# Attention stage: four PSUM banks for the scores and three in the ring of units, in place of three and four

## What is computed

```python
qkv = einsum('bnc,dc->bnd', xn, qkv_w) + qkv_b       # q, k, v: 16 heads of 32
attn = softmax(einsum('bhqd,bhkd->bhqk', q, k) * 32**-0.5)
out = einsum('bhqk,bhkd->bhqd', attn, v)             # then the output projection
return x + attention(xn) + experts(xn)
```

## Time and profile before

| | us |
|---|---|
| median of three runs | 4841.46 |
| the profiled execution, its own time | 4836.55 |
| span of its trace | 4834.7 |
| TensorE matmul, busy | 4691.4 (97%) |
| VectorE, busy | 3170.4 (66%) |
| ScalarE, busy | 2398.9 (50%) |
| GpSimd, busy | 3223.0 (67%) |
| mean granted TensorE clock | 0.987 |

### The profile page before, as it was taken

One profiled execution on the slowest core, in us unless ns is written; L12 is line 12 of the kernel. 1 busy time (PEld: TensorE's weight loads), 2 busy tenths in 40 slices (PEclk: granted clock), 3 DMA queues, 4 the chain that ended last, 5 costly groups with the idle time before them and its releaser, 6 DMA issues. The chain is left out here.

```text
span 4834.7 us, 66456 instructions
## 1 busy us (share of the span) xinstructions
PE 4691.4 (97%) x24396; PEld 2773.0 (57%) x24396; DVE 3170.4 (66%) x5296; ACT 2398.9 (50%) x4653; POOL 3223.0 (67%) x1117
## 2 busy tenths in 40 slices
PE   8999999999899999999999999999999999999979
PEld 6887878878654444444444444444444444444447
DVE  4223232333188888888888888888888888888534
ACT  2111121121146666666666666666666666666621
POOL 1121212121249998989989989999899998998920
PEclk9999999999979999999999999999999999999989
DMA  5344343343346655656656566665665656655466
GB/s 172 103 127 122 109 138 102 119 129 111 91 106 130 137 127 125 138 125 137 133 124 139 124 131 136 126 139 120 132 137 124 140 125 132 137 124 121 90 225 236
DMA packets 254215, 633.49 MB, mean 131 GB/s; under 512 B 45252, under 2 KB 79044, under 8 KB 212936
## 3 DMA queue, kind: packets, MB, share of 16 engines
q0 software_dynamic: 36864, 268.45, 27.8%
q1 hardware_dynamic: 217032, 360.85, 27.0%
HBM read 224.96 MB, written 134.74 MB: 74 GB/s over the span
## 5 line engine op out<-in xcount | busy, mean ns | idle before, releaser
L927 DVE TENSOR_REDUCE unit_max<-mx_ps 128x1 f32<-128x512 f32 x4096 | 2535.2, 681 | 317.0 <-PE mx_ps L1002 310.9
L836 POOL TENSOR_TENSOR p_pair<-p_sb 128x2048 f32<-128x2048 f32 x512 | 2439.8, 4811 | 185.3 <-PE mx_ps L1026 128.3
L913 ACT ACTIVATE p_sb<-st_ps 128x512 f32<-128x512 f32 x4096 | 2061.9, 628 | 905.5 <-PE st_ps L1073 905.5
L1002 PE MATMUL mx_ps<-k_x,q_x 96*128 96x512 f32 x4096 | 1684.9, 415 | 21.5 <-DMA k_x<-k_lo_d 19.6
L1073 PE MATMUL st_ps<-q_x,k_x 97*128 97x512 f32 x4096 | 1607.8, 413 | 37.9 <-ACT p_sb L913 37.3
L1073 PEld LDWEIGHTS st_ps<-q_x,k_x 97*128 97x128 f32 x4096 | 770.3, 188 | 599.3 <-ACT p_sb L913 512.8
L1002 PEld LDWEIGHTS mx_ps<-k_x,q_x 96*128 96x128 f32 x4096 | 784.6, 192 | 456.7 <-DVE unit_max L927 234.3
L1014 PE MATMUL o_ps<-p_sb,v_sb 128*32 128x512 f32 x8192 | 986.8, 599 | 0.0
L285 POOL TENSOR_TENSOR h_lo<-h_f,h_hi 128x512 fp32r<-128x512 f32 x128 | 165.2, 1291 | 687.7 <-DVE h_hi L469 687.7
L1014 PEld LDWEIGHTS o_ps<-p_sb,v_sb 128*32 128x32 f32 x8192 | 214.0, 109 | 494.1 <-ACT p_sb L913 309.8
L469 DVE CAST h_hi<-h_f 128x512 fp32r<-128x512 f32 x128 | 55.0, 431 | 541.9 <-ACT h_f L342 541.9
(11 more groups left out here) (94 smaller groups left out, 3926.8 us busy)
## 6 DMA issues: line engine op xcount, KB each, us to landing
p_pair<-p_pair POOLq DMA_DIRECT2D x256, 1024.0 KB, 7.3
q_x<-q_hi_d SPq DMA_DIRECT2D x128, 256.0 KB, 8.6
k_x<-k_hi_d SPq DMA_DIRECT2D x68, 256.0 KB, 7.3
xt<-x SPq DMA_DIRECT2D x64, 256.0 KB, 2.7
stage<-w SPq DMA_DIRECT2D x32, 512.0 KB, 5.1
q_hi_d<-qk_hi SPq DMA_DIRECT2D x64, 256.0 KB, 3.0
q_lo_d<-qk_lo SPq DMA_DIRECT2D x64, 256.0 KB, 3.9
k_hi_d<-qk_hi SPq DMA_DIRECT2D x64, 256.0 KB, 2.6
```

Source lines behind the costliest of these rows:

```text
L836: pool.tensor_tensor(p_pair[:, slot, :, :], p_sb[:, n % SLOTS, :, :], p_sb[:, (n + 1) % SLOTS, :, :], ALU.add).then_inc(pair_done, 1)
L913: act.activation(p_sb[:, (L * G * KT + n) % SLOTS, h, :], st_ps[bank(g, m)][:, :], ACT.Exp, scale=SCALE).then_inc(exp_done, 1)
L927: dve.reduce_max(unit_max[:, n // 4, n % 4:n % 4 + 1], mx_ps[UNIT_PLACE[n] % RING][:, :], AX.X).then_inc(bank_read, 1)
L1002: pe.matmul(mx_ps[UNIT_PLACE[n] % RING][:, :], q_x[qc][0:R, h, t * P:(t + 1) * P], k_x[u][0:R, h, kc * 512:(kc + 1) * 512], start=True, st ...
```

## The change

`SB` goes from 3 to 4 and `RING` from 4 to 3. All bank numbers, places and waits are worked out from these two, so they change with them: a score waits for the exponential four scores back, a fill of the ring for the read three places back. `PLACES` goes from 68 to 69. `TURNED` stays 54. The two sums at the very end, which now fall into one bank, get a wait each in place of one for both.

```diff
-    SB = 3
-    RING = 4
+    SB = 4
+    RING = 3
@@
-                pe.wait_ge(bank_read, ALL_READS)
                 for i in range(NS):
                     if PARTS[i][3] >= NP:
+                        pe.wait_ge(bank_read, ALL_READS + PARTS_AT[PARTS_IN:].index(PARTS[i][3]))
                         sums(TURNS - 1, G - 1, i, PART_PLACE[PARTS[i][3]])
```

## The result

The changed kernel takes 4934.8 us (median of 4, 4932.8 to 4935.5) against 4843.3 us (4 runs by now, 4841.4 to 4845.5): 1.0187 times the time before, 95% interval 1.0174 to 1.0199, or +91.5 us. Forecast were 4930 us and +89.

A forecast was written before the change was run, and what follows sets the result against it. TensorE's queue, held by exponentials, sets the pace; with the ring of three, late units wait for VectorE's reads. At +1.42 us a group, plus first group, tail and start, +89 on 4841.5 gives 4930 us, range 4885 to 4965.

The forecast's parts named there:

- the first stretch: Stage's first 46 us, at granted clock 0.50, units waiting for reads: called hidden, with +1 us for some odd places.
- The fourth score bank: Scores stop waiting for exponentials: alone -0.09 us a block; V0-V1, its copy hidden, -0.62 us net with the ring of three.
- Items 1 to 3: U8 waits for the fifth read: +0.16 us in V1-V2, V4-V5, V6-V7; +0.23 in V2-V3, V3-V4; +0.53 in V5-V6.
- Item 4, the wrap: V7-V0: 68 fills are no multiple of three, so the ring holds two there and U5, U6 wait: +0.57 us.
- The price of a late release: From a read's end to the waiting unit's matmul: 0.13 us, plus 0.02 for what follows; bounds 0.06 and 0.25.
- The sum: 61 full groups at +1.42 us, 86.6; first group +2.1; +0.8 and -1.5 for the last two; start +1: 89 us.
- The end: Last two groups, few units, their end hanging on GpSimd: +0.8 us before, -1.5 at the end.
- A: Faster rival: the ring of three carries the reads' backlog, only the added score bank counts: -64 us, 4777 us; chance 0.06.
- B: Rival, slower by less: a release costs 0.06 us and the ring's wrap only one place: +23 us, 4864; chance 0.07.
- B': Rival, within 0.2% of no change: the copy of the output also comes off V7-V0; chance 0.02.
- C: Rival, slower by more: a release costs 0.25 us, 2.5 us a group: +155 us, 4996; chance 0.05.
- D: Clock rival: new stalls bring one block a group to the lower clock level: +233 us on top, 5163; chance 0.02.

The follow-up runs named there:

- experiment 3: Changed kernel with VectorE reading 256 of a unit's 512 columns and the exponentials at a tenth of the scale: 4763.7 us, 0.9844 of the kernel before.
- experiment 4: Kernel before the change, with VectorE reading 256 of a unit's 512 columns and the exponentials at a tenth of the scale: 4822.8 us, 0.9960.
- Experiment 1: Changed kernel with three score banks again and the ring still of three, one PSUM bank idle: 4948.6 us, 1.0220 times the kernel before.
- Experiment 7: Changed kernel with two buffers for the units' maxima, VectorE's small reduction moved behind the eighth read: 4913.5 us, 1.0148 times the kernel before.
- Experiment 2: Changed kernel with ring banks numbered through all groups, so that no place is skipped between groups: 4914.0 us, 1.0150 times the kernel before.
- experiment 6: Changed kernel with ScalarE's copy of the output moved from ahead of the exponential of score 3 to that of score 8: 4935.2 us, 1.0194.
- experiment 5: Kernel before the change, with ScalarE's copy of the output moved from ahead of the exponential of score 3 to that of score 8: 4792.0 us, 0.9898.

## Why the prediction was right, point by point

- *What bounds the stage.* Right: TensorE's own queue, held by exponentials before and by reads after. Experiments 3 and 4 show that reads took no part in the pace of the groups before and set it after; in the first stretch, where a unit waits for every read the earlier trace rows, they set it before too.
- *The fourth score bank.* Right in both parts. U1 to U6 now run unhindered outside V7-V0, and V0-V1 gave back 0.64 us, forecast 0.62. Experiment 1 adds what the prediction said only by its sums: where the ring holds, the exponentials' pace costs nothing, so that bank is worth 0.07 us a group here and not the 1.14 that it is worth when reads are quick.
- *Items 1 to 3.* +0.16, +0.23 and +0.53 a block stood in the working; +0.15 to 0.17, +0.24 and +0.55 came. Experiment 7 isolates what V5-V6 had beyond a plain block: 0.38 us a group.
- *Item 4, the wrap.* +0.57 forecast, +0.58 measured; U5 and U6 stood at 2.68 and 3.27 where 2.75 and 3.34 were forecast. Experiment 2 takes it away and gets back the 0.35 that it is worth over a block behind a Z.
- *The price of a late release.* The sum was right and its split was not, in V4-V5 as an example. U8 starts 0.05 us behind R5's end, not 0.13; but V then follows U8 by 0.42 us and not by 0.34. From the end of the read to V there are 3031.64 - 3031.17 = 0.47 us, and 0.13 + 0.02 + 0.34 = 0.49 were assumed. The start of a matmul's entry was the wrong mark; the next instruction's start is the one that counts.
- *The sum.* A group came to +1.44 for +1.42: 61 of them 87.7 us for 86.6 (87.2 in the trace, from the first to the last of their V); the first group +2.1 for +2.1. The first stretch was mis-sized: from the first U to the first V it took 58.9 us for 54.8, +4.1 in place of +1. In the changed kernel's reads gaps of 0.29 us stand in it that the kernel before has not:

```profile
1337.64 4.87 DVE L927 TENSOR_REDUCE unit_max<-mx_ps 128x1 f32<-128x512 f32 x8 [0.29 <-PE mx_ps L1002]
```

  I had called it hidden, and did not look for the places where the first fills skip some. How the 4.1 us split over them was not tried. Experiments 6 and 7, with the same banks, took 60.0 and 59.9 us for that stretch. The granted clock is 0.50 in most of it, and rises 50.9 us behind the first U before the change and 55.2 after.
- *The end.* The last two groups were put at -0.7 us and came to +0.9. Their V do come sooner, the last by 4.0 us, yet GpSimd's last chain does not, as the prediction's sum had it: from the last V to the last Z it is 19.0 us for 13.8 before, and from there to the end of the span 207.7 for 4834.7 - 4626.7 = 208.0. The gather that precedes that last Z ended 1.3 us before it in both kernels, not 2; it costs nothing all the same.
- *How near the total came.* From the first unit to the end the two traces differ by 4.1 + 2.1 + 87.2 + 0.9 = 94.3 us, where 89 were forecast: the mechanism holds, and the first stretch is the term that was too small. That the medians differ by 91.5, nearer to the forecast, is luck: the runs of one kernel scatter by up to 4 us. The two profiled spans differ by 98.4; 4.0 of these lie before the first unit, in a stage that the change doesn't touch, and the profiled execution of the kernel before was 6.7 us below the median of its runs, that of the changed one 0.1 above its own.
- *The rivals.* A needed reads at most 0.52 us apart; they were 0.597, and experiment 3 supplied the condition. B, B' and C fell with the price of a release and with the wrap. D did not occur: the granted clock is 1.00 up to the last group. There one V is slow in each of the two kernels (3.16 us after, 3.47 before), so that this is no part of the loss.

## What to carry to other kernels

Where a producer issues in bursts, a ring is sized for the burst and not for the mean: count how far the reader lags at the burst's last item, by the timeline, and the item that reuses the bank is held by that read. Before a scarce buffer is given to a wait, look at what the waited-for engine does first; here one instruction's place in ScalarE's queue bought 48 us where moving a bank cost 91. And when a ring's size changes, see whether it still divides the round's items.

## What the runs showed of the hardware that was not expected

In the last group, where TensorE has only scores, values and sums, its granted clock falls for short stretches. There a V, 1.92 us elsewhere, can take 3 us and more. In the changed kernel it is one V, behind scores of which the fifth waited 2.01 us for ScalarE:

```profile
4662.03 1.92 PE L1014 MATMUL o_ps<-p_sb,v_sb 128*32 128x512 f32 x16
...
4667.11 1.96 PE L1073 MATMUL st_ps<-q_x,k_x 97*128 97x512 f32 x4 [2.01 <-ACT p_sb L913]
4669.01 3.16 PE L1014 MATMUL o_ps<-p_sb,v_sb 128*32 128x512 f32 x16
```

In the kernel before the V at the same place takes 3.47 us, behind an idle of 1.71 us. The same V is slow in experiments 1 to 4 (2.99 to 3.64 us, behind idles of 1.72 to 3.22). It is 1.92 or 1.93 us in experiments 5 and 6, where the copy stands later in ScalarE's queue and the idle is 0.22 and 0.53. But it is 1.92 in experiment 7 too, behind an idle of 2.03, so the idle alone does not decide it.

With four score banks no further V is slow. With three, further ones are, without a long idle: none in the kernel before, one in experiment 4, two in experiment 5 and four in experiment 1. These four, 1.4 to 1.6 us longer each than a quick one, make up nearly all of the 6.1 us by which its last group is longer than in the kernel before. Two of them in a row, behind a quick one (timeline), and the window around them (length, busy times, then the granted clock):

```profile
4699.86 1.92 PE L1014 MATMUL o_ps<-p_sb,v_sb 128*32 128x512 f32 x16
...
4705.28 3.54 PE L1014 MATMUL o_ps<-p_sb,v_sb 128*32 128x512 f32 x16
...
4712.38 3.53 PE L1014 MATMUL o_ps<-p_sb,v_sb 128*32 128x512 f32 x16
```
```profile
4700.00:4720.00 20.00, 19.33 (x76) 5.97 (x74) 0.26 (x1) 12.52 (x26) 14.94 (x5) 0.81 0.57 120
```

A mean of 0.81 lies between the two levels, 1.2 and 2.4 GHz, and the slow V take nearly twice the time. Ahead of each of these V stand eight scores, five of them held back by ScalarE, 0.22 us before the fourth; ahead of the quick ones between them stand the same. With units in between, in the steady groups of the changed kernel, new stalls of up to 0.5 us (U8 of V5-V6) left the clock at 1.00. The Trainium skill, TensorE: Matmul & The Clock Gate, section "A second HAM failure mode: psum-queue depth-cycling", describes such a swing for a kernel with short idles between groups of matmuls; of the groups here only the last shows one. Why the same group kept its clock for more blocks in the kernel before than in experiment 1, with the same three score banks, was not tried and stays open.
